# The multiply that scales a condition tile before it is rounded: on ScalarE instead of VectorE

## What is computed

```python
c = x @ W.T + 2.0 * lora(x, gates)              # condition, 512 features a token
c = c * rsqrt(mean(c * c) + 1e-6) * rms_weight
s = max(max|c| / 127, 1e-8);  q = round(c / s)   # quantise each token
gate, up = (q @ Wgq.T) * s * wsg, (q @ Wuq.T) * s * wsu
h = silu(gate) * up                              # 1376 features
s2 = max(max|h| / 127, 1e-8); q2 = round(h / s2)
out = (q2 @ Wdq.T) * s2 * wsd
```

## Time and profile before

| | us |
|---|---|
| median of 3 runs (lowest, highest) | 427.91 (427.58, 428.31) |
| the profiled execution | 427.92 |
| its span, first to last instruction | 425.6 |
| TensorE matmuls busy | 389.1 (91%) |
| TensorE weight loads busy | 310.1 (73%) |
| VectorE busy | 279.3 (66%) |
| GpSimd busy | 182.9 (43%) |
| ScalarE busy | 168.0 (39%) |

### The profile page before, as it was taken

One profiled execution on the slowest core, in us unless ns is written; L12 is line 12 of the kernel. 1 busy time (PEld: TensorE's weight loads), 2 busy tenths in 40 slices (PEclk: granted clock), 3 DMA queues, 4 the chain that ended last, 5 costly groups with the idle time before them and its releaser, 6 DMA issues.

```text
span 425.6 us, 6207 instructions
## 1 busy us (share of the span) xinstructions
PE 389.1 (91%) x2081; PEld 310.1 (73%) x2086; DVE 279.3 (66%) x464; ACT 168.0 (39%) x289; POOL 182.9 (43%) x155
## 2 busy tenths in 40 slices
PE   3989999999999999999999999996949859899993
PEld 2777888888888889888888888885837635455542
DVE  4757644444453477555555538658997998999993
ACT  4436443333332344333333313423511345466652
POOL 3777877777110322111211000085445542657461
PEclk9999999999999999999999999999969887999999
DMA  7866534545332768455556300524613350001002
GB/s 293 272 183 226 191 130 136 157 156 155 113 99 75 271 241 315 165 182 185 182 183 231 105 0 0 181 98 134 223 47 103 99 182 2 0 25 52 25 25 74
DMA packets 21677, 58.67 MB, mean 138 GB/s; under 512 B 3665, under 2 KB 6277, under 8 KB 21529
## 3 DMA queue, kind: packets, MB, share of 16 engines
q1 hardware_dynamic: 16833, 46.99, 32.3%
q0 software_dynamic: 4384, 10.62, 8.4%
q10 hardware_dynamic: 440, 0.79, 0.5%
HBM read 56.28 MB, written 2.12 MB: 137 GB/s over the span
## 4 chain that ended last, share of the span: by engine, by line
PE 73%; DVE 14%; issue 6%; POOL 2%; ACT 2%; DMA 2%; SPq 0%; DVEq 0%; ACTq 0%; POOLq 0%
PE ps L1220 27%; PE ps L1263 14%; PE ps L1442 8%; PE ps L1226 7%; PE ps L1256 4%; PE ps L1338 3%; PE ps L1479 3%; POOL agu L407 2%; DVE x_hl L812 2%; PE ps L1211 2%; PE ps L1273 1%; DVE cw L1083 1%; DMA agu<-a_gu_dram,idx_a 1%; DVE wq L1014 1%; DVE qs L1091 1%
## 5 line engine op out<-in xcount | busy, mean ns | idle before, releaser
L1220 PE MATMUL ps<-x_hl,wg_hl 128*128 128x512 f32 x528 | 127.5, 390 | 0.1
L1220 PEld LDWEIGHTS ps<-x_hl,wg_hl 128*128 128x128 f32 x528 | 97.6, 188 | 20.4 <-issue 1.1
L420 POOL DMA_INDIRECT b_raw<-b_gu_dram,idx_all x44 | 45.8, 1042 | 79.1 <-DVE b_hl L812 68.4
L902 DVE TENSOR_TENSOR act_raw<-ps,sil 128x512 f32<-128x512 f32 x22 | 15.2, 691 | 87.4 <-issue 59.2
L1263 PE MATMUL ps<-act_hl,wd_hl 128*128 128x512 f32 x264 | 64.0, 391 | 0.0
L1263 PEld LDWEIGHTS ps<-act_hl,wd_hl 128*128 128x128 f32 x264 | 48.2, 188 | 9.1
L475 POOL TENSOR_TENSOR t_raw<-t_raw,inv_b 128x1376 f32<-128x1376 f32 x8 | 25.8, 3239 | 61.6 <-DMA inv_b<-scale_scratch 49.7
L1442 PE MATMUL ps<-wq,qt 128*128 128x459 bf16 (+1 forms) x192 | 42.3, 375 | 4.1 <-DVE cw L1083 4.1
L1226 PEld LDWEIGHTS ps<-tg_hl,b_hl 128*128 128x128 f32 x264 | 37.2, 190 | 4.5 <-issue 1.2
L1226 PE MATMUL ps<-tg_hl,b_hl 128*128 128x256 f32 x264 | 38.4, 282 | 0.8 <-DVE tg_hl L812 0.8
L486 POOL TENSOR_TENSOR g_sb<-g_sb,u_sb 128x459 f32<-128x459 f32 (+1 forms) x24 | 27.6, 1164 | 26.6 <-ACT g_sb L740 26.5
(11 more groups left out here) (156 smaller groups left out, 600.5 us busy)
## 6 DMA issues: line engine op xcount, KB each, us to landing
wg_raw<-w_gu_dram SPq DMA_DIRECT2D x22, 512.0 KB, 4.8
nat<-w_nat_dram SPq DMA_DIRECT2D x11, 768.0 KB, 4.3
wd_raw<-w_d_dram SPq DMA_DIRECT2D x22, 256.0 KB, 2.7
t_raw<-wg_t_dram SPq DMA_DIRECT2D x4, 688.0 KB, 5.8
t_raw<-wu_t_dram SPq DMA_DIRECT2D x4, 688.0 KB, 5.4
t_raw<-wd_t_dram SPq DMA_DIRECT2D x5, 512.0 KB, 3.6
out_dram<-r_sb SPq DMA_DIRECT2D x7, 256.0 KB, 2.0
vu_raw<-w_vu_dram SPq DMA_DIRECT2D x3, 512.0 KB, 9.5
```

What stands on the lines that cost most here:

```text
L420: gp.indirect_dma_start(out=b_raw[:, slot, g, :], out_offset=None, in_=a["b_gu"], in_offset=bass.IndirectOffsetOnAxis(ap=idx_all[:, f, 2 * ...
L1220: mm(bank[:], wg_hl[:, slot, w, gu * H + k * P:gu * H + (k + 1) * P], x_hl[n][:, v, k, :], start=(k == 0 and (w, v) == THREE[0]), stop=False)
```

## The change

The instruction at L1097 is taken out of VectorE's loop. ScalarE's `q1_round(t)` now waits for the factor of its tile (`s_step`), does the same multiplication and addition in place on `cw`, signals `q1_scaled` itself, waits for that, and then subtracts ROUND as before. What is computed is the same.

```diff
             def q1_round(t):
-                act.wait_ge(q1_scaled, t + 1)
+                act.wait_ge(s_step, 4 * (t + 1))
+                nc.scalar.activation(cw[:, t % 3, :], cw[:, t % 3, :], ACT.Copy, bias=ROUND,
+                                     scale=qs[:, 6, t:t + 1]).then_inc(q1_scaled, 1)
                 if t >= 4:
                     act.wait_ge(qt_ready, t - 3)
+                act.wait_ge(q1_scaled, t + 1)
                 nc.scalar.activation(q1[:, t % 4, :], cw[:, t % 3, :], ACT.Copy, bias=-ROUND).then_inc(q1_made, 1)
...
                 if u >= 0:
                     dve.wait_ge(s_step, 4 * u + 3)
                     V.tensor_tensor(qs[:, 6, u:u + 1], qs[:, 5, u:u + 1], qs[:, 2, u:u + 1], ALU.mult).then_inc(s_step, 1)
-                    dve.wait_ge(s_step, 4 * u + 4)
-                    V.tensor_scalar(cw[:, old, :], cw[:, old, :], qs[:, 6, u:u + 1], ROUND, ALU.mult,
-                                    ALU.add).then_inc(q1_scaled, 1)
```

More of the change, by code:

```diff
@@ L1066, in _ @@
                 u = t - 1
-                cur, old = t % 3, u % 3
+                cur = t % 3
                 if u >= 0:
```

## The result

| | before | after |
|---|---|---|
| median of 20 runs (lowest, highest), us | 427.5 (425.91, 429.44) | 425.48 (424.12, 427.77) |
| ratio of the times, 95% interval | | 0.9953 (0.9937 to 0.9969) |
| span of the profiled execution, us | 425.6 | 423.7 |
| VectorE busy, ScalarE busy, us | 279.3, 168.0 | 274.1, 173.7 |

The kernel is faster by 2.0 us (1.3 to 2.7). The forecast was 425.0 us with a range from 423.5 to 426.9.

A forecast was written before the change was run, and what follows sets the result against it. TensorE was taken to wait at the end of the condition stretch for a ring of GpSimd's and VectorE's instructions. 427.92 - 2.55 (ring) - 0.4 (clock) = 424.97, so 425.0 us, range 423.5 to 426.9.

The forecast's parts named there:

- The ring: Condition stretch: GpSimd's power and product, then VectorE's L1097, t_round and cw, then power again; 4.8 us a turn, forecast about 4.3.
- who stands still: In five turns the stall beside GpSimd's product moves from L1097 to t_round, taking 2.6 to 2.9 us; L1071 not held.
- The length of the held t_round: VectorE's t_round of 1024 columns ends 0.50 us behind GpSimd's product, gaining 0.51 us a turn, 2.55 in all.
- The literal reading of full blocking: Held t_round takes its whole 0.68 us behind GpSimd's product, gaining 1.65 us in all; within a rival of chance 0.18.
- Three unheld multiplications: VectorE's other three L1097 cost about 0.40 us each; removing them leaves 1.2 us idle, as VectorE waits for TensorE.
- ScalarE and the loads at nothing: ScalarE's eight added multiplications, 0.722 us each by the nearest row, and SyncE's loads of the next pieces cost 0.
- The rival with ScalarE on the path: Each tile waits for ScalarE's longer instruction instead of VectorE's, costing 1.9 us: 429.8 us; chance 0.02.
- The clock at -0.4 us: TensorE's half-speed stretch at its first MLP matmuls shrinks by 0 to 1.8 us, saving 0.4 us (0 to 0.9).
- the sum: Whole kernel: the profiled execution's 427.92 us, less 2.55 for TensorE's earlier start and 0.4 for its clock, gives 424.97.

The follow-up runs named there:

- e3b: Kernel before the change, with GpSimd's six products of the down weights cut to one column each (their scaling left out); ratio to before 0.9733.
- e2: Kernel before the change, with only the last three multiplications (tiles 5 to 7) moved to ScalarE; ratio to before 1.0005.
- e5: Changed kernel with 18 extra matmuls, never read, in TensorE's idle time ahead of its first L1442; ratio to before 0.9926.
- e3a: Changed kernel with GpSimd's products of the down weights cut to one column each (their scaling left out); ratio to before 0.9742.
- e4: Changed kernel with VectorE's loop reordered: cw and small instructions beside GpSimd's product, t_round behind them; ratio to before 0.9851.
- e6: e4 with 10 extra matmuls on TensorE ahead of its first L1442; ratio to before 0.9856.

## Why the prediction was right, and where it was off

- *The ring and who stands still: right.* Held L1097 replaced by held t_round, L1071 (now L1074) not held, GpSimd first in every turn. So the engines do not meet only at semaphores, as the description of the core ahead of the prediction has it: no semaphore explains these stalls, and e3b shows that they end with the product. The Trainium skill, "SBUF — State Buffer", section "Who interferes with whom", names `tensor_scalar` among those that can take the ports shared with GpSimd, and says that the order of issue, not the shape, decides who waits. The trace agrees for the one order that the stretch has: GpSimd came first, and its product of 1024 columns kept its 2.4 us in every kernel that has it; no turn of the stretch has the other order.
- *The length of the held t_round: mis-sized.* 0.50 us behind the product was taken between two rows of other sizes; 0.55 was measured. The gain of a turn was 1.01 - 0.55 = 0.46 us, not 0.51 (0.42 to 0.47 by the starts of cw), and that of five 2.25 us, not 2.55. The literal reading of full blocking would have given 1.65.
- *Three unheld multiplications: right.* 0.40 us each reached gu_out (28.03 - 25.78 = 2.25 us for TensorE, 32.77 - 29.28 = 3.49 for VectorE), and VectorE then waits there; in e2 they leave TensorE's start where it was, and its ratio shows no gain (1.0005).
- *ScalarE and the loads at nothing: right here.* ScalarE took 0.723 us an instruction, as the earlier trace rows had it, and was never held; GpSimd waited for no load in the stretch. But the cover is thin: in e5 and e3a, where TensorE is faster at the end of the stretch, the last tile waits 1.21 and 0.75 us behind it. The rival with ScalarE on the path was thus a real mechanism, in its place at the last tile rather than at cw. The Trainium skill, "ScalarE: Activation LUTs", section "Rules for kernel authors", prefers VectorE for a multiplication. Where GpSimd holds nobody the profiles agree with it, by 0.8 us at L1118 (e3b against e3a), though the medians do not part the two; where GpSimd does hold VectorE the runs speak against it.
- *The clock at -0.4 us: too much.* TensorE sat idle 4.98 us where 4.8 was forecast, the clock fell again as forecast, and half speed ended 0.2 us sooner after the start of work, worth 0.1. The 4.2 to 6.0 us that the prediction allowed for the return were also too narrow below: later profiles have 2.8.
- *The end: a shift that the sum did not have.* At L1118 the gain is 41.94 - 39.59 = 2.35 us, and at L1164, VectorE's scaling of the last tile of h, it still is. ScalarE's rounding of that tile then starts 1.00 us behind L1164 against 0.72 before, with nothing in the trace that it waits for, so that at the last instruction of VectorE the gain is 98.70 - 96.64 = 2.06 us. The 0.3 us come back behind it: from its end to the end of the span it is 4.39 us against 4.70. The rows are these, before and after:

```profile
414.24 1.07 DVE L1164 TENSOR_SCALAR h_rnd<-g_sb,qs 128x768 f32<-128x768 f32 x2
414.96 1.44 ACT L747 ACTIVATE q<-h_rnd 128x768 bf16<-128x768 f32 x2 [1.95 <-DVE h_rnd L1164]
```
```profile
412.36 1.06 DVE L1164 TENSOR_SCALAR h_rnd<-g_sb,qs 128x768 f32<-128x768 f32 x2
413.36 1.44 ACT L750 ACTIVATE q<-h_rnd 128x768 bf16<-128x768 f32 x2 [2.24 <-DVE h_rnd L1164]
```

This is no accident of one execution. In all five profiles in which ScalarE does all eight multiplications (after, e3a, e4, e5, e6) the distance is 1.00 us and the rest behind VectorE's last instruction 4.3 to 4.4; in the six others it is 0.71 to 0.72 and 4.6 to 4.7. Why was not tried and stays open; it cost nothing in the span.

The account is then this. Of the 2.95 us forecast, 0.3 failed to come from the ring and 0.3 from the clock. That leaves 2.35, and the two spans, counted from cw of tile 0, differ by 103.82 - 101.45 = 2.37 us. The medians differ by 2.0 (1.3 to 2.7): the remaining 0.35 us lies within that interval, and no run gives it a cause. The time came closer than the gain did, and part of that is luck: the forecast starts from 427.92, the median of 20 runs before was 427.50, and 0.4 us of the missing gain does not show for that reason.

What the clock does from run to run was seen in single profiles only. That it makes part of the spread of 3.5 us among the 20 runs before is likely and not shown.

## What to carry to other kernels

A stalled instruction is worth only what comes out of the ring behind it: when it goes, ask which one is held in its place, and price the difference of the two ends, not the stall. Here moving the work between engines gave 0.5%; moving the instructions that nobody holds under the product that holds the others gave 0.9% by itself and 1.5% with the move. And the engine that takes work over needs its cover checked at the last tile too, since the cover went as soon as something else got faster.

## What the runs showed of the hardware

- A held VectorE instruction ends earlier behind GpSimd's product than its own length: 512 columns 0.27 us behind (0.487 alone), 1024 columns 0.55 (0.68), 1376 columns 0.74 (0.87).
- A tensor_tensor of 128x512 with one input in PSUM and one in SBUF took 0.69 us within GpSimd's product (e4), a 128x1 tensor_scalar 0.21 us. A small size is not enough for that: a tensor_scalar of 128x8 (L1046, at 307.37 in the kernel before) took 2.97 us beside a product of 128x1376.
- Half speed ended 2.8, 3.2, 3.5, 3.6, 5.7 and 5.9 us after the first L1442, in kernels that differ little; as work at half speed takes twice as long, half of the difference, some 1.5 us, is what a forecast can't tell for a single execution.
